# Attention's next batch made ready one slot ahead, K and Q relaid in six writes and four reads, and a gate product with tokens as weights

## The reference

```
def attention(x, c):                       # 16 heads of 16 channels
    q, k, v = Wq x + bq,  Wk c + bk,  Wv c + bv          # 256 x 512 per batch
    p   = softmax over s of (q_h^T k_h) / 4              # 512 x 512 per head
    out = p v, heads side by side
    return Wo out + bo

def experts(x):                            # 2048 tokens of 512, 12 experts, top 2
    probs = softmax(x @ gate_w.T);  w, i = top_k(probs, 2);  w = w / sum(w)
    return sum over the two of  w * ((silu(x @ w1[e].T) * (x @ w3[e].T)) @ w2[e].T)

x = x + tanh(g_xattn) * attention(layernorm(x), ctx)
x = x + tanh(g_ffn)   * experts(layernorm(x))
```

## Time and profile before

| | us |
|---|---|
| timed runs (3): median | 808.91 |
| lowest, highest | 804.32, 809.18 |
| the profiled execution | 802.83 |
| its span | 801.1 |
| mean granted clock of TensorE | 0.903 of full |

### The profile page before, as it was taken

The page is one execution under the profiler, slowest core; times in us unless marked ns, Lnnn a source line. Parts: engine busy times, 40 slices in busy tenths (PEclk is TensorE's granted clock), DMA queues, the critical chain, the costliest instruction groups (busy, mean ns, idle before and its releaser), DMA issues.

```text
span 801.1 us, 14200 instructions
## 1 busy us (share of the span) xinstructions
PE 621.2 (78%) x4169; PEld 270.8 (34%) x4170; DVE 420.0 (52%) x769; ACT 332.0 (41%) x394; POOL 243.0 (30%) x186
## 2 busy tenths in 40 slices
PE   3418849889698897988976523179999999999993
PEld 1101202213122131322311101156666666666661
DVE  4787546667466574657646652944333333333330
ACT  5216637567565666665684200002222222222221
POOL 5203105133141332314202111324444333544322
PEclk9959969999999999999997755569999999999997
DMA  5686886967949688695894747527587776764533
GB/s 159 172 221 179 209 248 172 217 205 194 274 134 249 184 179 256 151 275 165 181 283 150 209 152 262 211 79 208 121 234 201 225 205 185 196 114 83 91 40 41
DMA packets 75374, 146.54 MB, mean 183 GB/s; under 512 B 10757, under 2 KB 36870, under 8 KB 73798
## 3 DMA queue, kind: packets, MB, share of 16 engines
q1 hardware_dynamic: 43664, 68.18, 31.4%
q10 hardware_dynamic: 22038, 55.35, 22.7%
q0 software_dynamic: 9632, 22.55, 14.9%
HBM read 87.85 MB, written 53.74 MB: 177 GB/s over the span
## 4 chain that ended last, share of the span: by engine, by line
PE 43%; DMA 19%; issue 16%; DVE 8%; POOL 5%; SPq 5%; ACT 1%; POOLq 0%; DVEq 0%; ACTq 0%
PE S L1334 15%; PE O L1355 9%; DMA K<-k_parts 8%; PE O L1198 5%; PE MA L1234 4%; DMA out<-yo,slot_out 4%; SPq L480 3%; PE S L1159 3%; DMA zl<-osum 2%; PE S L1321 2%; PE MC L1234 2%; DMA q_parts<-qs 2%; ACT prob L694 1%; PE S L1345 1%; POOL qs L552 1%
## 5 line engine op out<-in xcount | busy, mean ns | idle before, releaser
L694 ACT ACTIVATE prob<-S 128x1024 f32<-128x1024 f32 x256 | 245.8, 1024 | 179.8 <-PE S L1159 146.7
L1334 PE MATMUL S<-W,xT 128*128 x1032 | 149.4, 302 | 1.2 <-DVE xT L1107 1.2
L1198 PE MATMUL O<-prob,V 128*32 128x512 f32 x1024 | 148.1, 642 | 0.0
L1159 PE MATMUL S<-Q,K 49*128 49x512 f16 x512 | 91.4, 406 | 65.4 <-DMA K<-k_parts 42.2
L1334 PEld LDWEIGHTS S<-W,xT 128*128 128x128 f16 x1032 | 99.9, 99 | 38.7 <-issue 1.5
L620 POOL DMA_INDIRECT out<-yo,slot_out x43 | 68.5, 1593 | 116.9 <-DMA out<-yo,slot_out 60.0
L1355 PE MATMUL O<-W,hT 128*128 (+1 forms) x344 | 90.3, 381 | 0.9 <-DVE hT L1127 0.9
L1159 PEld LDWEIGHTS S<-Q,K 49*128 49x128 f16 x512 | 20.2, 94 | 193.6 <-ACT prob L694 135.4
L1115 DVE SCALAR_TENSOR_TENSOR hh<-S,act 128x320 f32<-128x320 f32 x43 | 21.1, 492 | 122.6 <-PE S L1334 122.6
L798 DVE SCALAR_TENSOR_TENSOR wp<-wf,wp 128x1024 f16<-128x1024 f32 x48 | 69.6, 1451 | 1.7
L552 POOL TENSOR_TENSOR cs<-ctx,cs 128x1024 f16<-128x1024 f32 x8 | 17.0, 2125 | 150.1 <-DVE cs L859 150.1
(11 more groups left out here) (153 smaller groups left out, 650.4 us busy)
## 6 DMA issues: line engine op xcount, KB each, us to landing
wf<-wall ACTq DMA_DIRECT2D x48, 512.0 KB, 7.1
weight_parts<-wp ACTq DMA_DIRECT2D x48, 512.0 KB, 4.7
W<-weight_parts SPq DMA_DIRECT2D x10, 2048.0 KB, 9.2
Q<-q_parts SPq DMA_DIRECT2D x48, 128.0 KB, 7.8
K<-k_parts SPq DMA_DIRECT2D x48, 128.0 KB, 8.2
ctx<-ctx_in SPq DMA_DIRECT2D x8, 512.0 KB, 12.5
residual<-x SPq DMA_DIRECT2D x8, 512.0 KB, 13.9
k_parts<-ks SPq DMA_DIRECT2D x8, 512.0 KB, 2.8
```

Source lines behind the costliest of these rows:

```text
L694: act.activation(prob[:, u % RING, :], S[u % 2][:, :], ACT.Exp, scale=SCALE).then_inc(g.exp, 1)
L1159: last = pe.matmul(S[u % 2][:, s * T:(s + 1) * T], K[par][r0:r0 + PARTS * DK + 1, 2 * g4 + n, st * P:(st + 1) * P], Q[par][r0:r0 + PARTS * ...
L1198: last = pe.matmul(O[g4 % 2][2 * DK * j:2 * DK * (j + 1), :], V[par][:, st, GH * g4 + j, :], prob[:, u % RING, (j % 2) * T:(j % 2 + 1) * T ...
L1334: last = pe.matmul(ps, xT[par][:, xp * TT + k, :], W[:, bass.ds(off + (w * WCOL + (2 * k + n) * F), F)], start=(k == 0 and (xp, w) == (0, 0)),
```

## The change

- **One slot ahead.** A new flag `p` (t = 0 to 6): SP loads batch t+1 in slot t; VectorE takes its statistics behind step 6 (`LN_AT`), normalises behind step 8 (`XN_AT`) and casts its context behind step 11 (`CS_AT`); POOL makes the low parts in the same slot, the one of xs behind that of os, the one of cs at the very end. Batch 0 is done so ahead of slot 0.
- **Extras.** k0, k1, q0, q1 now stand at steps 0 to 3; the values are four pieces v0 to v3 of half the width (4, 5, 6, 10); o1 is in two halves (8, 9); o0 is at 7; t0, t1, lg stay at 12, 13, 14; lt is gone.
- **Relaying.** The DRAM copy holds the three parts in the order of the stack: three writes of 256 KB for each of K and Q, with runs of 2 KB, the high ones issued before the low part is there, and two reads of 384 KB each, with runs of 2 KB. The heads are grouped differently for that (`head`), and Wo is loaded in eight blocks.
- **Gate product.** The transposed tokens are the weights and the 12 gate columns move, so the result comes out with tokens in the partitions.
- **Part c.** The inverse sums are taken at step 1 (before: ahead of step 0), the product with them at step 5.
- **Quarters.** None in slot 0, 4 in slot 1 (behind 4, 7, 11, 13), 6 in slots 2 to 7 (behind 2, 4, 7, 11, 12, 13), 8 in slot 8, none in slot 9 or in the expert tiles.
- The constant rows that only the guarded run needs are no longer written in the normal run, POOL makes its constants after batch 0's low parts, and an exponential's table is loaded early.

```diff
-        EXTRA = {3: "k0", 4: "k1", 5: "q0", 7: "q1", 8: "o0", 9: "v0", 10: "o1", 11: "v1", 12: "t0", 13: "t1",
-                 14: "lg", 15: "lt"}
-        ON_AT, XN2_AT, SPLIT_AT = 6, 11, 6
+        EXTRA = {0: "k0", 1: "k1", 2: "q0", 3: "q1", 4: "v0", 5: "v1", 6: "v2", 7: "o0", 8: "o1a", 9: "o1b",
+                 10: "v3", 12: "t0", 13: "t1", 14: "lg"}
+        ON_AT, LN_AT, XN_AT, XN2_AT, CS_AT, SPLIT_AT = 5, 6, 8, 10, 11, 3
+        KQ_WRITES, KQ_READS = 16 * 2 * PARTS, 16 * 4
...
         def quarters(t):
-            if t.i is None and t.add == 0:
-                steps, experts = (4, 8, 11, 12), (0,)
-            elif t.i is None and t.add == 1:
-                steps, experts = (0, 2, 4, 6, 8, 10, 12, 14), (1, 2)
...
+            if t.i is None and t.add in (0, B + 1):
+                return []
+            if t.i is None and t.add == 1:
+                steps, parts = (4, 7, 11, 13), [(At(None, 0, 0), c) for c in range(4)]
...
             else:
-                steps, experts = (0, 5, 9, 12), (t.before(-1),)
+                steps = (2, 4, 7, 11, 12, 13)
...
         # SyncE
-                    if a:
-                        wait(sp, g.xc, t, 32, 0, s_bog)
-                        wait(sp, g.a_free, t, NA, -NA)
-                        load_batch(t, par)
+                    if p:
+                        nxt = t.before(-1)
...
+                        wait(sp, g.cl, nxt, 1, -1)
+                        load_ctx(nxt, 1 - par)
+                        load_x(nxt)
...
-                        wait(sp, g.kl, t, 1, 1)
-                        sp.dma_start(k_dram.rearrange("h (m p) t -> p h m t", p=P), ks[:, :, :, :]).then_inc(g.qkst, 16)
-                        wait(sp, g.ql, t, 1, 1)
-                        sp.dma_start(q_dram.rearrange("h (m p) t -> p h m t", p=P), qs[:, :, :, :]).then_inc(g.qkst, 16)
+                        for stack, parts, dram, hi, lo, order in ((K, ks, k_dram, g.kh, g.kl, (0, 0, 1)),
+                                                                  (Q, qs, q_dram, g.qh, g.ql, (0, 1, 0))):
+                            wait(sp, hi, t, 1, 1)
+                            for r in sorted(range(PARTS), key=lambda r: order[r]):
+                                if order[r] == 1:
+                                    wait(sp, lo, t, 1, 1)
+                                sp.dma_start(dram[:, r], parts[:, order[r]].rearrange("p m t -> p (m t)"))\
+                                    .then_inc(g.qkst, 16)
...
-                        for s in range(2):
-                            for r, (qp, kp) in enumerate(((0, 0), (1, 0), (0, 1))):
-                                for stack, dram, part in ((Q, q_dram, qp), (K, k_dram, kp)):
-                                    src = dram[part].rearrange("(g s c) t -> s c g t", s=2, c=DK)[s]
-                                    sp.dma_start(stack[par][64 * s + DK * r:64 * s + DK * (r + 1), :, :], src)\
-                                        .then_inc(g.qk, 16)
+                        for stack, dram in ((K, k_dram), (Q, q_dram)):
+                            for s in range(2):
+                                sp.dma_start(stack[par][64 * s:64 * s + PARTS * DK, :, :]
+                                             .rearrange("p (g m) t -> p g (m t)", m=CT),
+                                             dram.rearrange("(g s) r c n -> s (r c) g n", s=2)[s]).then_inc(g.qk, 16)
         # GpSimd
                     if a:
-                        lo_part(t, cs, ctx_sb[par], g.ch, g.cl)
...
-                        lo_part(t, xs, xn, g.xh, g.xl)
                         lo_part(t, ks, kf, g.kh, g.kl)
+                        lo_part(t, qs, qf, g.qh, g.ql)
                     if c:
+                        lo_part(bc, os_, on, g.oh, g.ol)
+                    if p:
+                        inverse_spread(nxt, mv, veps, rstd, g.mv, g.veps, g.rstd)
+                        lo_part(nxt, xs, xn, g.xh, g.xl)
+                    if c:
+                        inverse_spread(bc, mv2, veps2, rstd2, g.mv2, g.veps2, g.rstd2)
                         wait(pool, g.x2h, bc, 1, 1)
                         pool.tensor_tensor(xs2[:, 1], xn2[:, :, :], xs2[:, 0], ALU.subtract).then_inc(g.x2l, 1)
+                    if p:
+                        lo_part(nxt, cs, ctx_sb[1 - par], g.ch, g.cl)
         # TensorE
-                            last = pe.matmul(MC[0:NE, 0:C], gate[:, k, :], xT2[:, :, k * P:(k + 1) * P],
-                                             start=(k == 0), stop=(k == TT - 1))
+                        for m in range(CT):
+                            for k in range(TT):
+                                last = pe.matmul(MC[:, m * NE:(m + 1) * NE], xT2[:, m, k * P:(k + 1) * P], gate[:, k, :],
+                                                 start=(k == 0), stop=(k == TT - 1))
```

411 lines of the change are left out of this document (216 added, 195 removed).

## The result

The changed kernel takes 824.91 us (median of 4, 821.99 to 825.12) against 809.04 us (median of 4, 804.32 to 810.97) for the kernel before on the same chip: ratio 1.021, 95% interval 1.016 to 1.026. It is slower; I had predicted 785, with a range of 760 to 810. The profiled execution has a span of 823.1 us, 22.0 more than before; the medians are only 15.9 apart, because the profiled execution before was 6 us quicker than its own median.

A forecast was written before the change was run, and what follows sets the result against it. It took attention's chain of waits, not a full engine, as the bound. Terms -16.2, -12.7, +8, 0, -1, -2 sum to -23.9: 779 us from the profiled 802.83, stated as 785 against the timed median 808.91, range 760 to 810.

The forecast's parts named there:

- term 3: Slots 2 to 6: gains outweighed by six quarters' waits at the slot's end, +1.6 us each, +8 together.
- third rival: Slots 2 to 6: POOL delays the fourth quarter, next slot starts at slow clock; +7.5 a slot, 821 us, chance 0.12.
- the walk: Middle slot summed event by event from its first exponential: 50.0 us against 48.4, bounds -3.4 and +10.
- Term 1: Slot 0: no weight quarters, earlier last Q write, four cheaper reads of 2 KB runs: -16.2 us.
- Its rival: K and Q reads: relaying no cheaper, so slot 0 gains only 12 us, middle-slot loads land later; 794 us, chance 0.13.
- Term 2: Slot 1: the 11.64 us K wait goes, four quarters fewer, slow clock costs +1: -12.7 us.
- Term 4: The rest: slot 7 unchanged (0), slot 8 -1 us, tail -2 us without two quarters before o0's evacuation.
- Signs I had named: Trace signs, such as first exponential near 39 us; slot 0 above 44 or middle slots above 54 would show it wrong.
- term 1's best case: Slot 0: lower bound of its change, reads at the full fast rate of 4.2 us, given as -19 us.

The follow-up runs named there:

- E12: Changed kernel with POOL's two low parts at a slot's end covering 32 of 512 columns of each block (work left out): 816.6 us, ratio 1.012.
- E2: Changed kernel with a third buffer for loaded weight quarters, at their own steps, so loads go out three quarters ahead: 806.4 us, ratio 0.998.
- E15: Changed kernel with a third buffer for loaded quarters and its six quarters behind steps 0, 2, 4, 7, 9, 13: 788.2 us, ratio 0.980; again 791.5, 0.983.
- E13: Kernel before with only the new quarter plan, nothing else of the change: 880.1 us, ratio 1.092.
- E7: Changed kernel with K and Q read back in 8 transfers of 1 KB runs instead of 4 of 2 KB: 821.3 us, ratio 1.018.
- E3: Changed kernel with the whole quarter plan of the kernel before, everything else of the change kept: 799.8 us, ratio 0.989.
- E14: Changed kernel with its six quarters behind steps 0, 2, 4, 7, 9, 13, two load buffers as before: 797.9 us, ratio 0.989.

## Why the prediction was wrong

**The step that failed** is term 3, "+1.6 each" for slots 2 to 6; they took +8.7. The mechanism was named (fourth quarter late behind POOL, sixth quarter's load behind its store, ScalarE waiting), and the third rival priced it at +7.5, with a chance of 0.12. The sizes in the walk were wrong, all in one direction. From the slot's first exponential, predicted and measured in slot 5:

- end of the cast of xs, 34.2 and 36.8. The walk has k0 and k1 at full clock and adds 0.8 for the slow one at the end. It was 1.8: 2.74 us for k0's products instead of 1.47, and 1.60 for the value products behind them instead of 1.07; step 1 took 5.4. Step 6 took 4.1 (4.7 on the mean of slots 2 to 6; the walk has 2.2 and a stall of 1.4), with ScalarE idle for 2.13 us at its end, issuing the second quarter's store and the load behind it.
- fourth quarter ended, 39.0 and 43.0. I allowed 1.5 us for the collision between bounds of 0 and 3.4; it was 3.1, in each of slots 2 to 6 (2.02 + 3.03 against 1.92). POOL's two low parts start behind two casts that VectorE itself makes just before, so the overlap isn't chance but order. The Trainium skill bears on this (SBUF — State Buffer, Who interferes with whom): a VectorE cast or tensor-scalar in its two-port mode, and a VectorE operation with two inputs in SBUF, contend with a GpSimd operation that reads SBUF; for the two-port mode it says that whoever issues first has the ports for the whole instruction and the other is fully blocked. The rows agree: POOL's starts at 303.29 and ends at 305.86, VectorE's is issued at 303.91 and ends at 306.94, its own time behind.
- the sixth's load, 6.5 and 8.4 us (bounds 5.3 to 11.2).
- the end of the slot, 50.0 and 56.0.

The bounds in a row reached +10 and the truth was +8.7. For each I had taken something near the good end, and as they stand in a row the errors added. The collision was the smallest part of it: without it (E12) a slot takes 0.8 to 1.2 us less, and slot 7 took +6.4 almost without one. Two quarters for one pair of buffers within two steps, and the late load that comes of it, are the larger part: a third buffer (E2) gives 3 to 4 us, other steps and the third buffer (E15) 5.8 of the 8.7.

**Term 1** (-16.2, was -9.3): the last Q write landed at 33.8 and not at 31.5. It went out at 29.3, near E13's 28.7, but the last of the six takes 4.5 us to land where one of two takes 2.8, which I hadn't counted. The reads took 12.1 us from their first issue, not 7.5. I took the rate of the stretch of the earlier trace rows for the reads' own, and put its difference to the earlier trace rows down to run size. E7 shows that it isn't that. The fast stretch held loads and stores of 128 partitions. In the changed kernel the same pair of stretches is

```profile
298.00:308.00 10.00, 6.38 (x48) 1.97 (x47) 9.26 (x10) 5.04 (x6) 5.75 (x3) 0.99 0.94 189
308.00:316.30 8.30, 7.85 (x52) 2.95 (x50) 2.00 (x4) 3.88 (x4) 0.00 (x0) 0.80 1.05 395
```

with 2 KB runs in the reads of the first, and still 189. Of the rule that I set aside (the Trainium skill, DMA: Bandwidth & Descriptors, the summary table: full rate from 512 B up), this much stood: from 1 to 2 KB nothing is gained. The full rate the reads didn't reach with either. Its rival's -12 was nearer. And the cause of the gain was another one: the quarters' traffic beside the reads, which the sum didn't have at all. Without it the kernel before wins 6.4 us in the reads and 2.8 in front of them (E13), as much as the changed kernel does.

**Term 2** (-12.7, was -11.9) came out, with luck. No wait for K is left behind slot 0, as I said; but I gave the whole 11.64 us of it to the early q1 and about 2 us to four quarters less. By the square above, the early q1 and the rest without the new plan bring 1.0 us in slot 1 (E3), four quarters less without them 6.4, with the wait for K down to 1.22 (E13). Two things were late there side by side, and only taking both away gives the 11.9.

**Term 4**: slot 7 was not the same for want of a next batch; it has the same six quarters and took +6.4. Slot 8 held. The tail gave 6.9 instead of 2, and not where I had it: from the last exponential to the issue of its last write it takes 34.8 us, 34.7 before, so the two quarters counted for nothing. The write lands in 5.0 us instead of 8.1, and the routing's first instruction on VectorE comes 3.9 us behind that instead of 7.4, which no run explains.

**Gate product**: I said eight products at 1.0 to 1.6; there are sixteen, and they take 1.95 us at full clock (E15's rows) and 3.59 at the slow one in the tail, against 1.68 for the old ones, which needed a transpose back as well.

**Signs I had named**: first exponential near 39, no (46.6, above my limit of 44); fourth quarter above 1.23, yes; ScalarE idle with VectorE waiting for a load just before, yes; PE clock under 1 at slot starts, yes; no wait for K behind slot 0 and slot 1 near 43, yes; middle slots above 54, yes.

Two sums of the prediction are off without weight for the outcome: the third rival's parts give +10.5 and not +12, and term 1's best case (31.5 + 1.8 + 4.2) is -17.7 and not -19.

Open: how the rest of the change comes to save 8.5 us in a middle slot under the new plan when it saves none under the old one (by steps, 2.8 us of it lie in steps 0 to 5 and 5.0 in steps 6 to 12; four of E13's six quarters meet POOL, two of the changed kernel's). Half open: what keeps six quarters at 51 us in E15 when four take 48.4. Against E3, 2.2 of the 2.7 us stand in step 3 with its late row sums; no run takes that wait away by itself.

## What to carry to other kernels

When work is moved from one stage to another, price it in the new place by its chain: which buffer must be free, which queue holds the instruction that frees it, and what stands behind that instruction. Three pieces of work behind three steps in a row, in two pairs of buffers, made a change slower that was worth a percent otherwise; other steps for the same work (E14) turned 2.1% slower into 1.1% faster. When two things are late side by side, as in slot 1, taking one away shows little of what it costs. And take a DMA rate only from transfers that reach the same partitions.

## What the runs showed of the hardware

DMA engines with a busy share of 0.94 to 1.14 moved anything from 115 to 395 GB/s. The rate did not go by runs of 1 or 2 KB (162 and 170), but along with the partitions of a transfer (16: 115 and 124; 48 in one half: 162 and 170, and 189 with some of the quarters' traffic in the stretch; 128: 395). One of the two instructions that split a quarter on VectorE, 0.69 or 1.23 us by itself, waits for the end of a POOL subtraction that it starts beside and then takes about its own time (2.0 to 2.5 and 3.0 us), and POOL's own goes from 2.13 to 2.5 us where VectorE came first. A DMA of 32 KB among others at 373 to 417 GB/s came late enough to hold VectorE for 1.0 to 3.1 us; at 47 to 124 GB/s it did not. Around a wait of TensorE of 6.83 us, which ended at 265.0, its granted clock was 0.50 from 263.9 to 270.0, and six products of 128x512 took 2.74 us instead of 1.47.
